# Cross-attention and FFN on one core: the V products of the 2nd and of the last head group stand in one piece each

## Reference

```python
qh = (layernorm(x) @ Wq.T)   # split into 16 heads
kh = (ctx @ Wk.T)
vh = (ctx @ Wv.T + bv)
scores = einsum('bhsd,bhtd->bhst', qh, kh) * scale
probs = softmax(where(mask, -inf, scores))
out = einsum('bhst,bhtd->bhsd', probs, vh)
x = x + out @ Wo.T + bo
x = x + ffn(layernorm(x))
```

## Time and profile before

| | |
|---|---|
| median of three runs | 2721.75 us |
| span of the profiled execution | 2732.2 us (45231 instructions); its time as a run is not listed apart, the slowest run took 2732.61 us |
| TensorE busy | 2611.6 us, 96% |
| VectorE busy | 1596.1 us, 58% |
| ScalarE busy | 1031.2 us, 38% |
| GpSimd busy | 840.9 us, 31% |
| mean granted TensorE clock | 0.978 of full speed |

### The profile page before, as it was taken

One profiled execution on the slowest core, in us unless ns is written; L12 is line 12 of the kernel. 1 busy time (PEld: TensorE's weight loads), 2 busy tenths in 40 slices (PEclk: granted clock), 3 DMA queues, 4 the chain that ended last, 5 costly groups with the idle time before them and its releaser, 6 DMA issues. The chain is left out here.

```text
span 2732.2 us, 45231 instructions
## 1 busy us (share of the span) xinstructions
PE 2611.6 (96%) x14258; PEld 1943.7 (71%) x14258; DVE 1596.1 (58%) x3166; ACT 1031.2 (38%) x1903; POOL 840.9 (31%) x1559
## 2 busy tenths in 40 slices
PE   7999999999999999999999949999999999999998
PEld 5676667667766766776676537888888888888887
DVE  4675676667667666766765474444444444444454
ACT  2433433343343334334433454333333333333332
POOL 1643654474356346445644600000000000000000
PEclk9999999999999999999999868999999999999999
DMA  4344254344435433533444240000000000000000
GB/s 149 84 123 124 68 148 116 91 102 130 117 75 141 116 104 89 141 113 82 128 116 112 52 156 16 31 31 31 31 31 31 31 31 31 31 31 31 31 31 31
DMA packets 125252, 215.58 MB, mean 79 GB/s; under 512 B 20244, under 2 KB 22292, under 8 KB 124709
## 3 DMA queue, kind: packets, MB, share of 16 engines
q1 hardware_dynamic: 121124, 214.14, 28.0%
q10 hardware_dynamic: 4096, 1.06, 0.2%
HBM read 79.86 MB, written 33.55 MB: 42 GB/s over the span
## 5 line engine op out<-in xcount | busy, mean ns | idle before, releaser
L742 ACT ACTIVATE probs<-bank 128x512 f32<-128x512 f32 x640 | 359.2, 596 | 316.0 <-PE bank L534 310.7
L1159 PE MATMUL y_bank<-projT,a_hi 128*128 128x512 f32 x1024 | 409.1, 399 | 0.0
L1147 PE MATMUL h_bank<-x2T_hi,fcT 128*128 128x512 f32 x1024 | 406.4, 397 | 0.9 <-ACT scale_row L1230 0.9
L1148 PE MATMUL h_bank<-x2T_lo,fcT 128*128 128x512 f32 x1024 | 406.9, 397 | 0.0
L1161 PE MATMUL y_bank<-projT,a_lo 128*128 128x512 f32 x1024 | 403.9, 394 | 0.0
L1074 POOL COPY x_res<-x_in_sb 128x512 f32<-128x512 f32 x64 | 53.7, 879 | 1030.4 <-DVE y_sb L1376 967.9
L1238 ACT ACTIVATE relu<-h_bank,scale_fc 128x512 f32<-128x512 f32 x256 | 175.9, 687 | 503.5 <-PE h_bank L1151 503.5
L1349 DVE CAST a_hi<-act_sq 128x512 fp32r<-128x512 f32 x256 | 120.8, 472 | 372.5 <-ACT act_sq L1243 372.5
L435 POOL TENSOR_SCALAR_AFFINE_SELECT probs<-probs 128x256 f32<-128x256 f32 (+1 forms) x640 | 228.1, 367 | 250.8 <-ACT probs L742 244.4
L509 PE MATMUL bank<-stack 96*128 96x512 f32 (+3 forms) x1024 | 268.9, 340 | 19.5 <-DMA stack<-stage 15.5
L534 PE MATMUL bank<-stack 98*128 98x512 f32 (+3 forms) x1024 | 267.4, 346 | 17.0 <-DMA stack<-m_stage 15.9
(11 more groups left out here) (187 smaller groups left out, 4922.1 us busy)
## 6 DMA issues: line engine op xcount, KB each, us to landing
stack<-stage SPq DMA_DIRECT2D x768, 128.0 KB, 2.3
xc_rows<-in_x_dram SPq DMA_DIRECT2D x16, 1024.0 KB, 5.3
x_res<-in_x_dram SPq DMA_DIRECT2D x16, 1024.0 KB, 5.5
x<-x_res SPq DMA_DIRECT2D x64, 256.0 KB, 2.2
x_in_sb<-x SPq DMA_DIRECT2D x16, 1024.0 KB, 5.6
out_dram<-y_sb SPq DMA_DIRECT2D x64, 256.0 KB, 2.0
xc_rows<-in_ctx_dram SPq DMA_DIRECT2D x15, 1024.0 KB, 5.3
stack<-m_stage ACTq DMA_DIRECT2D x128, 8.0 KB, 2.2
```

Source lines behind the costliest of these rows:

```text
L742: act.activation(probs[:, s[2], :], t_bank[u % 2][:, :], ACT.Exp, scale=SCALE).then_inc(exp_done, 1)
L1147: pe.matmul(h_bank[b % 2][:, :], fcT[:, k, cols], xT_hi[:, k, :], start=k == 0, stop=False)
L1148: pe.matmul(h_bank[b % 2][:, :], fcT[:, k, cols], xT_lo[:, k, :], start=False, stop=False)
L1159: pe.matmul(y_bank[j][:, :], a_hi[:, b % RING, P * j:P * j + P], projT[:, b, :], start=b == 0, stop=False)
```

## The change

The list of batch_steps is written in another order at two places; nothing else differs.

```diff
-        ("PV", 1, 0), ("NM", 0, 0), ("STACK", 3, 1), ("SEND", 2), ("XT", 1), ("PV", 1, 1), ("PV", 1, 3), ("XT", 2),
-        ("PV", 1, 2), ("T", 2, 0), ("XT", 3), ("S", 3, 0), ("NH", 0, 0), ("T", 2, 1), ("T", 2, 2), ("NC", 1),
+        ("XT", 1), ("PV", 1, 0), ("NM", 0, 0), ("STACK", 3, 1), ("SEND", 2), ("PV", 1, 1), ("PV", 1, 3),
+        ("PV", 1, 2), ("XT", 2), ("T", 2, 0), ("XT", 3), ("S", 3, 0), ("NH", 0, 0), ("T", 2, 1), ("T", 2, 2), ("NC", 1),
...
-        ("NL", 2, 0), ("OA", 2, 1), ("CT", 0), ("CT", 1), ("PV", 3, 3), ("PV", 3, 2), ("NT", 3), ("NR", 3),
-        ("NB", 3), ("NM", 3, 0), ("NH", 3, 0), ("NM", 3, 1), ("OC", 0), ("NL", 3, 0), ("K", 0), ("NH", 3, 1),
+        ("PV", 3, 3), ("NL", 2, 0), ("PV", 3, 2), ("OA", 2, 1), ("NT", 3), ("NR", 3), ("NB", 3), ("CT", 0),
+        ("NM", 3, 0), ("CT", 1), ("NH", 3, 0), ("NM", 3, 1), ("OC", 0), ("NL", 3, 0), ("K", 0), ("NH", 3, 1),
```

## The result

The changed kernel takes 2740.26 us (median of eight runs) beside 2723.41 us for the kernel before in the same series: a ratio of 1.0055, 95% interval 1.0040 to 1.0070, that is 15 us slower (11 to 19). 2739.9 was predicted, in a range of 2725 to 2756.

A forecast was written before the change was run, and what follows sets the result against it. TensorE, busy 96% of the span, was taken as the bound. K0's wait 15.0, last batch -0.2, group 1's V products 0 and clock falls 3.3 gave +18.1 on 2721.75: 2739.9 us, range 2725 to 2756.

The forecast's parts named there:

- K0's wait: At group 3's V products: K0 waits for CT's low parts, 1.0 us per batch, 15.0 us in 15.
- The transfers are issued at about 488.25 instead of 487.95, and T(2,0) starts 0.3 to 0.4 later: At group 1's V products: XT1's high part on ScalarE delays the transfers of the maxima, T(2,0) by 0.3 to 0.4 us.
- The sum for place one: At group 1's V products: TensorE's saving becomes a longer wait for the maxima, the rest hides under the stack wait; 0.
- I take two more: Behind group 1's V products: two more drops of the granted clock to 0.50, +3.3 us.
- the rival with the clock unchanged: At group 1's V products the clock falls no oftener than now: 2736.6 us, chance 0.25.
- The total idle of the place grows little: At group 1's V products: the reason given for clock falls staying near the present two, with +3.3 us taken.
- The last batch: It has no K0 and no transposes: one piece less, two switches of 0.1, -0.2 us.
- some 10.2: Last batch of the profiled execution before: us lost in 20.3 us at clock 0.50, taken as absent from the median run.
- The rival that switches are worth more than the waits: At both reordered stretches: six fewer narrow-to-full switches of 0.1 us per batch, 9 us in 15; 2712.8 us, chance 0.10.

The follow-up runs named there:

- Place two alone: Only the new order at the V products of group 3, against the kernel before: 2743.28 us, ratio 1.0057.
- place one alone: Only the new order at the V products of group 1, against the kernel before: 2744.01 us, ratio 1.0058.
- with the ones products early: ONES 1 moved ahead of S(3,0); ratios to the kernel before: 1.0022 in the whole change, 0.9970 with only group 1's V products reordered.
- the two kernels with many falls: Only group 1's order changed, ratio 1.0058; whole change with OA(2,1), CT0, CT1 ahead of group 3's V products, 1.0038; both against the kernel before.

## Why the prediction was right, and where it was not

- **K0's wait** (1.0 us in 15 batches): right, step for step. From the first V product of group 3 the prediction had CT0 at 5.29, the first high part at 5.92, the first low part at 6.55, the second at 7.38 and K0 at 8.05; measured 5.24, 5.87, 6.51, 7.31 and 8.05. (The V products of before begin at 518.07, that is K0 at 525.22 less 7.15.) The 0.10 for the product that starts after a wait is 0.12, by the way from K0 to the next transpose (56.07 less 55.95). Place two alone shows its 15.5 us, the whole change against place one alone, both with the ones products early, 14 us. TensorE's idle is 1.08, longer than K0's delay of 0.90, since TensorE is done with OC0 0.18 earlier than before.
- **"The transfers are issued at about 488.25 instead of 487.95, and T(2,0) starts 0.3 to 0.4 later"**: wrong. The issue waits for VectorE's low part alone and not for ScalarE's copy ahead of it; T(2,0) starts as early as before, and its wait is 0.77, not 1.2, S(3,0)'s 0.88, not 0.4. The sum for place one, 0 by its waits, still held, since the stack's transfer ends the place in either order.
- **"I take two more" falls, +3.3 us**: wrong for the whole change, which has two, as before. The other steps give +14.8, so the rival with the clock unchanged (2736.6) is what happened; the measured difference of 15 us is its difference. That 2740.26 stands so near to 2739.9 is luck: 3.3 us that were not there stand in for 1.7 by which the median of before was taken too low (2723.41 in the longer series) and for 2.0 by which the difference of the two medians, 16.85, is above 14.8.
- **"The total idle of the place grows little"**: this reason did not hold. At place one alone the same order has six falls for two, 16 us. In the whole change, whose batch place two makes longer, they stayed away. The prediction summed the two places, and the clock's part of the one depends on the other.
- **The last batch** (-0.2): not separable. It is 4.6 us shorter in the profiled execution of the changed kernel, where the clock fell for 3.4 us instead of 20.3; one execution each doesn't tell whether the order does that. It tells something else: 17 us less at half clock shortened that batch by 4.6 us, so the 20.3 us cost some 5 us and not the "some 10.2" by which the prediction explained why the profiled execution is above the median. The 10.2 us at half clock in batch 1 were overlooked there.
- **The rival that switches are worth more than the waits** was half right: with K0's wait taken away the batch is 0.25 shorter, but 0.25 in 15 batches are 4 us, not 9.

The Trainium skill, "TensorE: Matmul & The Clock Gate", section "HAM oscillation — how this bites in real kernels", has the clock fall over long waits for a transfer between bursts of products. The runs here show falls without one: in batches 2 to 15 of place one alone no wait between the transpose and S(3,0) is longer than 0.90 us, and the clock falls behind it in six batches of 14; filling the largest of these waits ended the falls.

**What stays open:** why at 94.5 to 94.9 us the changed order falls so much oftener than at 95.6 to 96. The runs show this for two groups of lengths only, and for waiting as well as for products; that the length as such decides is not shown. The traces hold a hint that was not followed: in the two kernels with many falls these begin within 0.7 us of S(3,0)'s start, in all the others 1.0 to 1.3 us behind it.

## What to carry to other kernels

The slack of a consumer (here 0.65 us before K0) comes from the work that stands between it and its producer. An order that takes this cover away to make another block denser pays for the copies that the cover had hidden (1.44 us of cover gone, K0 0.90 later), and filling the wait afterwards bought little here, where the next stage hangs on the same chain. Time each part of a change alone and together: where the clock falls in some batches and not in others, the parts need not add, and a part that "costs nothing" can cost as much as the whole. The cure was not the order itself but a block of independent products moved into the largest wait; it ended the falls of batches 2 to 15 under either order.

## What the runs showed of the hardware

- A DMA issue in ScalarE's program does not wait for the copy ahead of it to end: it began at 486.45 inside a copy that lasts from 486.15 to 486.75, 0.10 after the end of VectorE's part that it waits for. The same holds in all 15 batches: the issue comes 1.58 to 1.59 us after the transpose, while the copy runs from 1.29 to 1.88.
- The granted clock falls to 0.50 with waits of at most 0.9 us: six of batches 2 to 15 in place one alone, none of them when one of the waits was filled with 1.0 us of work. A fall of 3.4 us costs 1.6 us.
- How often it falls goes with the length of the repeated loop as well: place one's order has 6 and 9 falls with batches of 94.85 and 94.5 us, and 1 to 3 with batches of 95.6 to 96.0 (one execution each).
